# A Flamingo-like transformer on one core: first bias in a weight's freed last row, last rows and gathers moved into attention

## The reference, cut to what matters

```python
p = softmax(xt @ Wr + br); probs, idx = top_k(p, 2); probs = probs / probs.sum()
h = layernorm(relu(einsum('td,edf->etf', xt, W1) + b1), g1, be1)      # 128 -> 512
y = layernorm(relu(einsum('etf,efd->etd', h, W2) + b2), g2, be2)      # 512 -> 128
x = x + tanh(g_ffn[1]) * sum over the two chosen experts of share * y
```

## Time and profile before

| | us |
|---|---|
| median of 3 runs (lowest, highest) | 1903.54 (1902.86, 1907.15) |
| the profiled execution: own time | 1909.09 |
| the profiled execution: span in the profile | 1907.3 |
| PE busy | 1710.9 (90%) |
| DVE busy | 1166.0 (61%) |
| ACT busy | 778.5 (41%) |
| POOL busy | 761.2 (40%) |

### The profile page before, as it was taken

One profiled execution on the slowest core, in us unless ns is written; L12 is line 12 of the kernel. 1 busy time (PEld: TensorE's weight loads), 2 busy tenths in 40 slices (PEclk: granted clock), 3 DMA queues, 4 the chain that ended last, 5 costly groups with the idle time before them and its releaser, 6 DMA issues. The chain is left out here.

```text
span 1907.3 us, 30893 instructions
## 1 busy us (share of the span) xinstructions
PE 1710.9 (90%) x10309; PEld 1127.0 (59%) x10309; DVE 1166.0 (61%) x3041; ACT 778.5 (41%) x1965; POOL 761.2 (40%) x983
## 2 busy tenths in 40 slices
PE   5796698768899999999999997879999999999999
PEld 4544476535575657756577564546756565656656
DVE  6836666546756657657576564557757555554654
ACT  2411254315443646537466273126627422232222
POOL 3433545618746636656266462007647200000000
PEclk7865899889999999999999997989999999999999
DMA  8010022100000000000000000000000473643452
GB/s 299 1 28 13 27 81 70 40 17 15 9 1 1 2 1 1 1 1 2 1 2 1 1 2 1 1 1 1 1 1 2 133 204 120 201 120 113 130 168 84
DMA packets 62796, 90.40 MB, mean 47 GB/s; under 512 B 11056, under 2 KB 29104, under 8 KB 61872
## 3 DMA queue, kind: packets, MB, share of 16 engines
q1 hardware_dynamic: 60592, 84.23, 14.4%
q0 software_dynamic: 2048, 4.20, 0.8%
HBM read 78.43 MB, written 9.96 MB: 46 GB/s over the span
## 5 line engine op out<-in xcount | busy, mean ns | idle before, releaser
L1583 POOL TENSOR_TENSOR rows<-rows,rinv 128x512 f32<-128x512 f32 x192 | 197.1, 1054 | 139.6 <-DVE rinv L1821 139.6
L2492 ACT ACTIVATE region_b<-psum 128x512 f32<-128x512 f32 x132 | 78.8, 597 | 259.1 <-PE psum L2454 259.0
L1747 ACT ACTIVATE rows<-psum,nmax 128x512 f32<-128x512 f32 x192 | 130.2, 684 | 125.0 <-DVE nmax L1814 124.9
L2466 PEld LDWEIGHTS psum<-region_c,region_b 128*128 128x128 f32 x1024 | 132.1, 192 | 56.1 <-issue 43.4
L2530 DVE TENSOR_TENSOR region_b<-region_b,psum 128x512 f32<-128x512 f32 x128 | 87.9, 686 | 124.7 <-ACT region_b L2492 122.3
L1813 DVE TENSOR_REDUCE lg<-psum 128x2 f32<-128x1024 f32 x128 | 155.7, 1216 | 6.0 <-PE psum L1631 2.9
L1930 POOL TENSOR_TENSOR rows<-rows,rinv 128x128 f32<-128x128 f32 (+2 forms) x192 | 127.1, 683 | 77.4 <-DVE rinv L2099 77.4
L1825 DVE COPY turned<-psum 128x512 f32<-128x512 f32 x128 | 88.3, 690 | 92.3 <-PE psum L1643 92.0
L1631 PE MATMUL psum<-region_a,region_b 64*128 64x256 f32 x1024 | 134.0, 399 | 8.0 <-ACT rows L1747 5.6
L2094 DVE TENSOR_REDUCE nmax<-psum 128x1 f32<-128x128 f32 (+3 forms) x256 | 113.7, 486 | 42.4 <-PE psum L1976 41.4
L2466 PE MATMUL psum<-region_c,region_b 128*128 128x128 f32 x1024 | 133.5, 275 | 1.3 <-DVE region_b L2538 1.3
(11 more groups left out here) (752 smaller groups left out, 3600.4 us busy)
## 6 DMA issues: line engine op xcount, KB each, us to landing
pt<-gates SPq DMA_DIRECT2D x128, 128.0 KB, 3.0
ysb<-gates SPq DMA_DIRECT2D x128, 128.0 KB, 3.6
region_a<-in_eg SPq DMA_DIRECT2D x32, 256.0 KB, 3.4
region_a<-in_eu SPq DMA_DIRECT2D x32, 256.0 KB, 3.5
region_c<-in_weights SPq DMA_DIRECT2D x32, 256.0 KB, 4.7
sorted<-kctx SPq DMA_DIRECT2D x2, 1536.0 KB, 14.5
region_b<-sorted SPq DMA_DIRECT2D x12, 256.0 KB, 3.2
made<-rows SPq DMA_DIRECT2D x12, 256.0 KB, 2.4
```

Of the source, the lines that this page charges most:

```text
L1583: nc.gpsimd.tensor_tensor(row(u, j), row(u, j), rinv[:, 2 * u + j:2 * u + j + 1].broadcast_to([P, S]), ALU.mult).then_inc(s.pn, 1)
L1747: nc.scalar.activation(row(u, j), s_bank(u, j), ACT.Exp, bias=nmax[:, 2 * u + j:2 * u + j + 1], accum_out=sum_column(u // T, u % T, j)).th ...
L2466: mm = nc.tensor.matmul(bank(7)[:, P * t:P * (t + 1)], htb[:, i % 2, P * t:P * (t + 1)], wd, start=(i == 0 and t == 0), stop=(i == n_items ...
```

## The change

1. **b1.** Since the tokens' numbers sum to zero, the last row of W1 can be subtracted from the other 127, and that leaves the last row free; b1 takes its place, and the last number of each turned token becomes 1. `load_first_matrices` now loads rows 0 to 126 of each expert's W1, copies of its last row to 127 partitions (into parts of region_c and region_b), and b1 into row 127. POOL subtracts in the first block. `fold_b1` is gone, and ACT's copy of a turned quad is a plain copy of 127 rows.
2. **The first sort.** Its steps stand at 2n instead of n, and its 16 scatters are issued four to a step. The second sort's later steps come one earlier, its scatters three to a step.
3. **The pages.** The relu of a quad's rows moves from POOL to DVE, bias, centring and adding to other steps, a fourth hidden buffer is added, and the last quad's relu, norm and store move into attention_2 of batch 0 (`last_rows_1`).
4. **The combine.** Only batch 0's stays in the third block, one gather a step from step 33. Those of batches 1, 2 and 3 go into attention_2 of batches 0, 1 and 2, one gather a step in steps 1 to 8, and the three operations of the add one a step in 10 to 12.

```diff
         def load_first_matrices(sp, s):
+            lo = early_at["b1"][0]
             for e in range(E8):
-                sp.dma_start(w1[:, e, 0:F1], a["w1"][:, e, :]).then_inc(s.w1_in, 16)
+                sp.dma_start(w1[0:D - 1, e, 0:F1], a["w1"][0:D - 1, e, :]).then_inc(s.w1_in, 16)
+                sp.dma_start(last_row(e)[0:D - 1, :], a["w1"][D - 1:D, e, :].broadcast_to([D - 1, F1])).then_inc(s.w1_in, 16)
+            sp.dma_start(w1[D - 1:D, :, 0:F1], a["early"][0:E8, lo:lo + F1].rearrange("(o e) f -> o e f", o=1)).then_inc(s.w1_in, 16)
...
+                for e in range(E8):
+                    yield 20 + e
+                    if e == 0:
+                        pool.wait_ge(s.w1_in, 16 * (2 * E8 + 1))
+                    rows = w1[0:D - 1, e, 0:F1]
+                    nc.gpsimd.tensor_tensor(rows, rows, last_row(e)[0:D - 1, :], ALU.subtract)
...
-                for j in range(GT):
-                    yield step(10 + j)
-                    pool.wait_ge(s.r_slots, 1)
-                    for n in range(K1):
-                        at_slot = slots[:, g, GT * n + j:GT * n + j + 1]
+                for m in range(K1 * GT):
+                    j, n = m // K1, m % K1
+                    yield step(10 + m / per_step)
...
+                def rows_relu(q):
+                    dve.wait_ge(s.yb, 4 * (q + 1))
+                    nc.vector.tensor_scalar(page_y[q % 3], page_y[q % 3], 0.0, None, ALU.max).then_inc(s.yrelu, 1)
...
-                     [fold_b1(s_fold), front(sg, 3, bank(1), front_2, front_w2), route_1(sr, 0, bank(2), lambda n: n)], first_loads)
+                     [front(sg, 3, bank(1), front_2, front_w2), route_1(sr, 0, bank(2), lambda n: 2 * n, 4)], first_loads)
...
-            block_of(k, sync, main, [route_1(sr, 1, bank(7), lambda n: n),
-                                     combine_beside(combine_1(s1, 0, found_b[0]), 35, 37),
-                                     norm_ahead(s1, xs[0], ahead_w, bank(7), keys_of(0), 39, 42, LN_EPS),
-                                     combine_beside(combine_1(s1, 1, found_b[1]), 40, 44)])
+            route_at = (0, 0, 1, 2, 3, 4, 5, 6, 7, 8)
+            block_of(k, sync, main, [route_1(sr, 1, bank(7), lambda n: route_at[n] if n < 10 else n - 2, 3),
+                                     combine_beside(s1, 0, 33, 42),
+                                     norm_ahead(s1, xs[0], ahead_w, bank(7), keys_of(0), 43, 46, LN_EPS)])
...
-                        if late and 1 <= n <= 8:
-                            late[(n - 1) // 4].gather(pool, 2 * ((n - 1) % 4), 2)
+                        if combined and 1 <= n <= K1 * T:
+                            combined.gather(pool, n - 1)
...
-                        for i, batch in enumerate(late):
-                            if n == 4 * i + 6:
-                                batch.add(dve)
+                        if n > K1 * T + 1:
+                            next(added, None)
...
-                sp.wait_ge(s0.w1_in, 16 * E8)
                 sp.wait_ge(s0.rows_out, 32)
```

More of the change, by code:

```diff
@@ L45 @@
 FRONT_SMALL = 884
+HID = 4
 SH3 = 128
@@ L1207, in sync @@
             def sync(sp):
-                for q in range(n_quads + 5):
+                for q in range(n_quads + 4):
                     if 3 <= q < n_quads:
@@ L1360, in rows_add @@
                                                        op0=ALU.mult, op1=ALU.add).then_inc(s.yo, 1)
-                for k in range(n_pages + 8):
+                for k in range(n_pages + 4):
                     q = k // 4 - 1
@@ L1383, in gpsimd @@
                 rstd_link = chained(pool, s.yrstd)
-                for k in range(n_pages + 8):
+                for k in range(n_pages + 2):
                     q = k // 4 - 1
[L1386 to L1391, removed]
                     if k % 4 == 1 and 0 <= q < n_quads:
@@ L1466, in combine_beside @@
-        def combine_beside(c, gather_at, add_at):
+            return record(gather=gather, add=add)
+        def combine_beside(s, b, gather_at, add_at):
+            c = combine_1(s, b)
             def tensor(pe):
@@ L1475, in vector @@
                 yield add_at
-                c.add(dve)
+                yield from (add_at for _ in c.add(dve))
             def gpsimd(pool):
                 yield gather_at
-                c.gather(pool)
+                for stored_third in (s.out_0, s.out_1, s.out_2):
+                    pool.wait_ge(stored_third, 16 * (QUADS // 3))
+                for m in range(K1 * T):
+                    yield gather_at + m
+                    c.gather(pool, m)
             return record(tensor=tensor, vector=vector, scalar=scalar, gpsimd=gpsimd)
@@ L1492, in keys_of, with attention_2 @@
             return copy
-        def attention_2(k, b, late=()):
+        def attention_2(k, b, combined=None, last=None):
             s = sems(k % 2, ATTENTION_2)
@@ L1573, in _ @@
                     clear_set(sp, 1 - k % 2)
+                    if last:
+                        last.sync(sp)
                 @block.gpsimd
@@ L1578, in _ @@
                     nc.gpsimd.memset(vtok[0:2 * K, 4, :], 0.0).then_inc(s.zero, 1)
+                    if last:
+                        last.gpsimd(pool)
                     def normalise(u):
@@ L1766, in _ @@
                     copy_ctx(0, bank(4))
-                    for batch in late:
-                        batch.wait_stored(act)
+                    if last:
+                        last.wait_stored(act)
                     exps(0)
@@ L1793, in _ @@
                 def _(dve):
+                    rows = last.vector(dve) if last else iter(())
                     for c in range(PAIRS):
+                        next(rows, None)
                         dve.wait_ge(s.pq, 2 * c + 2)
@@ L1833, in _ @@
                     ctx_max(0)
+                    added = combined.add(dve) if combined else iter(())
                     for n in range(steps + 1):
```

165 lines of the change are left out of this document (89 added, 76 removed).

## The result

The changed kernel took 1984.1 us (median of 4 runs, 1981.53 to 1988.08), the kernel before 1905.35 (4 runs, 1902.86 to 1909.26): a ratio of 1.0413, with a 95% interval of 1.0384 to 1.0443. It is slower by 79 us; 1985 was forecast. The profiled execution took 1988.08, with a span of 1986.3.

A forecast was written before the change was run, and what follows sets the result against it. PE was busy 90% of the span, DMA engines full only in the first 40 us, with nobody waiting. 1909.1 + 127.3 - 9 - 25 - 12 = 1990.4, less 5.5 = 1985 us; range 1852 to 2010, likeliest case 1955 to 2010.

The forecast's parts named there:

- The load: First block: the 127-row loads and copies all run on one engine, 170 us, done at 201; block +127.3 us.
- The work queued behind: First block, POOL after the wait: 8 subtractions and 16 softmax operations, 25.2 us; block ends 10.3 us after them.
- Rival 1: First block: loads spread as before and the wait is nothing; whole 1859 us, range 1845 to 1885; chance 0.25.
- +1 us, at most +3: First block if loads spread: POOL's subtractions mostly hide in its gaps, so the block grows by only this.
- The second block: Second block: folding gone, POOL done at 223.5 instead of 227.6, shorter tail; gain 9 us, between 5 and 13.
- The third block: Third block: shorter PE waits and the relu off POOL; gain 25 us, 20 to 30.
- its three waits: Third block, PE's waits: second group's pages gain 5.5 us, the combine 8.2, the end 7.7.
- The 3.6 us that I gave the relu: Third block: relu leaves POOL, so DVE's scale comes sooner; some 0.3 us per quad, 12 quads.
- attention_2: attention_2, batches 0 to 2: 155.2 + 154.1 + 152.4 = 461.7 us against 473.7; gain 12.
- The rest: All blocks outside the first three and attention_2 of batches 0 to 2: forecast change 0.
- 17, 5, 5 and 23: Own range's parts in us: load 17 either way, blocks two and three 5 each, attention_2 up to 23.
- Rival 4: attention_2: PE's granted clock falls to 0.93 when adds stop it; costs 20 us, whole 2005; chance 0.03.

The follow-up runs named there:

- e1: Changed kernel with W1's loads cut into 112 and 15 rows and the last-row copies on 128 partitions: 1863.9 us, ratio 0.9768 to the kernel before.
- e2: Changed kernel with only the eight last-row copies on 128 partitions, the loads still of 127 rows: 1905.3 us, ratio 0.9985.
- e3: Changed kernel with both kinds of load cut into 122 and 5 rows: 1899.8 us, ratio 0.9965.
- e4: Kernel before, with each load of W1 cut into 127 rows and 1 row, nothing else: 1923.0 us, ratio 1.0075.
- e5: e1 run once more, unchanged, beside later runs as their measure: 1862.4 us.
- e10: e1 with the relu of the rows of all quads but the last back on POOL: 1866.6 us, ratio 0.9780.
- e8: e1 with attention_2's gathers two a step in steps 1 to 4 and the add in one go at step 6: 1891.1 us, ratio 0.9909.
- e12: e1 with attention_2's gathers still one a step, but each batch's add in one go at step 10: 1880.1 us, ratio 0.9842.
- e9: Changed kernel, 127-row loads kept, with the eight subtractions and their wait put behind the first block's softmax operations: 1955.8 us, ratio 1.0252.

## Why the prediction was right, and where it wasn't

**The load: right.** POOL asked at 69.4 and was let through at 198.3; 201 was forecast from 31 + 170. The choice was the step on which all hung, and rested on equal parts of a prime count; e1, e2, e3 and e4 show it from four sides. The price of 170 us was 167, from 31.5 to 198.3: 16 DMAs at nearly 10.5.

**The work queued behind: right in sum, with one term too small.** 24 operations were to take 25.2 us and took 25.9: a subtraction of 127x512 has 1.23 to 1.27 us, not the 1.05 of a softmax operation, whose second input is 16 numbers a row, repeated (that this is why was not tried). The tail had 9.4 us instead of 10.3. With the load over 2.7 us earlier, that makes the 3 us by which the block was shorter than forecast.

**Rival 1 was the time of another kernel.** With the loads spread it would have been 1859; e1 has 1863.9 and e5 1862.4. Most of that difference is the ground it was added to: the kernel before took 1907.2 and 1909.1 in those sets, not 1903.5. As changes, 44.5 us of gain were forecast and 43.4 and 46.7 measured. A term was still wrong, the first block's: "+1 us, at most +3" where e1 has +3.6 and e5 +6.0. Larger gains elsewhere covered it in e1 (attention_2 15.0 for 12), and that was luck. I had counted POOL's gaps as free. The 8 us gap lay beside VectorE's norm, and the two take turns: one of the norm's four operations to each subtraction of 1.23 us. The rule of the Trainium skill that I had used for the adds alone (SBUF — State Buffer, who interferes with whom) says also that VectorE's two-port modes lock the pair it shares with GpSimd, whoever issues first having it for the whole instruction. The rows agree in the times, 4.95 us beside the subtractions and 1.11 without; that the norm runs in such a mode no row says. It was to be applied wherever POOL's new work falls, not only where VectorE's does.

**The second block: right step by step.** The first softmax operation came 86.0 us after the block's start (85 forecast), POOL's last one ended 114.3 after it (114.3). The tail after it was 7.6 instead of 6, so the gain was 7.2 instead of 9, within its 5 to 13. (e1, with the same second block, has 119.4: a gain of 9.8.)

**The third block: right, somewhat undersized.** 29.0 against 25. The idle time of PE fell from 35.2 us to 10.5, by 24.7, and the forecast had 21.4 for its three waits: the second sort's is 3.8 for 2.4 (and another wait, by way of POOL's scatters and VectorE), the combine's 0 for 2.5, the end's 5.3 for 8. The other 4.3 us are PE's busy time at a granted clock of 0.97 instead of 0.90, a term that the forecast lacks. The same block took 128.9 to 136.7 over the kernels that have it unchanged, so the gain is 23 to 31, and the 4 us over my number are no finding. The 3.6 us that I gave the relu are not settled by e10, and the sum of idle time and clock leaves little room for them.

**attention_2: right.** 153.8, 151.3 and 153.0 against 155.2, 154.1 and 152.4. Of the 19.4 us that batch 0's gained, 9.2 are PE's busy time (158.0 to 148.8, the clock at 0.98 for 0.93). I had reckoned with the clock as a rival that would cost, not as a part of the gain. That the spreading is what saves was argued then and is shown by e8 and e12.

**The rest: not foreseen.** 6.5 us, of which 6.0 in the block after batch 2's attention, whose code is untouched (below); e1 took 197.8 us there and the kernel before 198.1, and e9, with the changed code, 196.6, so it goes with the execution rather than with the change. In the sum it made up for a first block that was 3 us shorter than forecast, and gains that were 6 larger in total; without it 1985 would have been 7 too high. That 1985 met 1984.1 to a microsecond is therefore luck; that the load would cost 170 us is not. Nor is the range's upper end well founded: the terms named beside it, 17, 5, 5 and 23, add up to 2035, not 2010.

**Rival 4** (PE's clock falls in attention_2): not seen; it rose there, to 0.98 in batch 0's.

## What to carry to other kernels

Before cutting a row off a tile, divide: a DMA of 128 rows ran on 16 engines, of 122 on two, of 127 on one, and 170 us of load are no longer hidden where 11 were. Cut such a transfer into 112 and 15 rows (e1), or load the 128th too and overwrite it later (not tried on W1 here). When pricing a slow transfer, go through two queues behind it, the issuing engine's own (e4: 7 us for a clearing that came too late) and that of the engine that waits (24 us of 124, e9).

## What the runs showed of the hardware

- A DMA engine that is behind holds up the issuing queue itself: each 127-row load kept SP for some 10.5 us, the time in which an engine moved 127 packets, while the DMA share of all 16 was 0.07. In e4 it was even the load of a single row that SP stood 9.7 us at, behind one of 127.
- POOL's operations with two inputs in SBUF stretched VectorE's norm from 1.11 to 4.95 us, four times over for four subtractions.
- PE's granted clock differs between executions in a block with the same code, and so does its length. The windows of the kernel before, for the block after batch 2's attention and 50 us within it, beside the two of the changed kernel above:

```profile
1061.00:1259.00 198.00, 162.98 (x992) 102.19 (x992) 120.03 (x353) 77.36 (x209) 70.07 (x102) 0.90 0.00 1
1160.00:1210.00 50.00, 44.09 (x177) 25.70 (x178) 21.80 (x86) 18.63 (x29) 4.38 (x9) 0.85 0.00 0
```

And 10 us from 120 us after the block's start, first in the kernel before, then in the changed one:

```profile
1181.10:1191.10 10.00, 10.00 (x49) 5.80 (x48) 4.39 (x17) 2.86 (x7) 0.00 (x0) 1.00 0.01 2
...
1252.00:1262.00 10.00, 10.00 (x25) 5.16 (x25) 2.47 (x13) 1.69 (x3) 0.00 (x0) 0.50 0.00 0
```

The whole block took 198.0 us at a granted clock of 0.90 before and 204.1 at 0.88 after; in the 50 us, for the same 44 us busy, 0.85 against 0.72 of 2.4 GHz. In the 10 us PE was busy throughout in both, at 2.4 GHz with 49 matmuls before, at 1.2 GHz with 25 after. Over all profiles of this study with that code it took 196.5 to 205.4. What PE did ahead of those stretches is alike in the rows (a wait of 7.4 us for VectorE), so what decides is open. It bounds what a single profile can say to some 9 us here.
